# A fused decoder layer on one core: the product with the inverted softmax sums moves from GpSimd to VectorE, and every engine's order is written anew

## The reference, cut to what matters

```
x = layernorm(x + self_attention(x))          # causal; scores from Q, W_cross, shift_weights and gate
x = layernorm(x + cross_attention(x, ctx))    # 112 x 375 scores per head, mask, softmax
x = layernorm(x + ffn(x))                     # ffn: gate, up (256 -> 704), silu(gate)*up, down (704 -> 256)

def fp4_linear(x, w):                         # every linear of the ffn
    return einsum(fp4_quant_dequant(x), fp4_quant_dequant(w))   # blocks of 16: scale = max|x|/6, round to the E2M1 grid
```

## Time and profile before

| what | value |
|---|---|
| median of 3 runs | 675.13 us (674.81 to 675.4) |
| the profiled execution | 676.12 us, of which the span of the core is 674.3 us |
| PE busy | 572.2 us, 85% |
| DVE busy | 537.2 us, 80% |
| ACT busy | 285.4 us, 42% |
| POOL busy | 235.5 us, 35% |
| mean granted TensorE clock | 0.948 of full |
| DMA | 76.95 MB, mean 114 GB/s |

### The profile page before, as it was taken

How to read it: one execution, slowest core, us unless ns; L and a number is a source line. 1 busy time by engine, 2 the same in 40 slices (tenths; PEclk the granted TensorE clock), 3 DMA queues, 4 the chain that set the end, 5 groups by cost and what they waited for, 6 DMA issues and landing times.

```text
span 674.3 us, 15980 instructions
## 1 busy us (share of the span) xinstructions
PE 572.2 (85%) x5410; PEld 360.8 (54%) x5410; DVE 537.2 (80%) x1443; ACT 285.4 (42%) x671; POOL 235.5 (35%) x312
## 2 busy tenths in 40 slices
PE   5876589799989898888989888887989898987875
PEld 3544255355655656565655655564656554544543
DVE  3498688775989979798988979566989887886784
ACT  2442155365345445344444545453444454434312
POOL 5352064352253505243341605242343516133100
PEclk9997699698999999899999989997999999998988
DMA  7566435354453535244452535353453525320000
GB/s 226 143 168 175 128 130 138 95 150 110 105 148 93 153 92 141 72 118 137 120 144 78 149 91 145 111 158 83 115 140 105 142 88 140 83 72 23 29 1 24
DMA packets 75808, 76.95 MB, mean 114 GB/s; under 512 B 13056, under 2 KB 67280, under 8 KB 75728
## 3 DMA queue, kind: packets, MB, share of 16 engines
q1 hardware_dynamic: 73488, 73.58, 40.0%
q10 hardware_dynamic: 2240, 2.35, 1.0%
HBM read 39.72 MB, written 27.00 MB: 99 GB/s over the span
## 4 chain that ended last, share of the span: by engine, by line
PE 40%; DVE 37%; issue 10%; POOL 5%; ACT 3%; DMA 2%; SPq 1%; DVEq 0%; POOLq 0%; ACTq 0%
PE misc L2251 14%; DVE junk L1447 5%; PE misc L2237 4%; PE score L2171 4%; PE prob L2185 4%; PE xpv L2226 3%; DVE qt L1359 3%; DVE qt L1363 3%; PE misc L2337 3%; DVE qt L1353 3%; DVE qt L1361 3%; DVE amax L1439 3%; DVE qt L1356 2%; POOL rstd L752 2%; PE prob L2180 2%
## 5 line engine op out<-in xcount | busy, mean ns | idle before, releaser
L1447 DVE CUSTOM_DVE_ANT_0 junk<-score,maskbias 112x375 bf16<-112x375 f32 x256 | 129.3, 543 | 57.1 <-PE score L2171 56.8
L947 ACT ACTIVATE xP<-prob 128x448 f32<-128x448 f32 (+1 forms) x192 | 95.2, 540 | 90.3 <-PE prob L2185 86.5
L2251 PE MATMUL misc<-wguT,xqT 128*128 128x352 f32 x224 | 81.7, 497 | 1.8 <-ACT xqT L907 1.1
L748 POOL TENSOR_TENSOR aattT<-anum,aden 128x224 f32<-128x224 f32 x16 | 10.6, 665 | 204.9 <-DVE aden L1486 196.1
L728 POOL TENSOR_TENSOR move_a<-mT,negeye 16x448 bf16<-16x448 f32 x64 | 63.5, 1014 | 48.5 <-ACT mT L907 48.5
L728 POOL TENSOR_TENSOR move_x<-mT,negeye 16x448 bf16<-16x448 f32 x64 | 61.2, 971 | 54.7 <-ACT mT L907 54.7
L752 POOL TENSOR_TENSOR rstd<-veps,half 128x1 f32<-128x1 f32 (+1 forms) x44 | 27.1, 621 | 108.1 <-DVE veps L1522 108.1
L2171 PE MATMUL score<-xK,xQ 64*128 64x375 f16 x256 | 45.6, 348 | 17.6 <-DVE xmax L1447 16.6
L2251 PEld LDWEIGHTS misc<-wguT,xqT 128*128 128x128 f32 x224 | 44.7, 206 | 25.0 <-issue 10.0
L2185 PE MATMUL prob<-move_x,shift_x 128*128 128x448 bf16 x192 | 54.8, 365 | 1.2 <-POOL move_x L728 0.9
L2226 PE MATMUL xpv<-xP,xV 128*32 128x112 f32 (+1 forms) x1536 | 54.5, 273 | 1.0 <-ACT xP L947 0.9
(11 more groups left out here) (157 smaller groups left out, 1094.2 us busy)
## 6 DMA issues: line engine op xcount, KB each, us to landing
xk_dram<-xk_parts SPq DMA_DIRECT2D x64, 192.0 KB, 3.2
xK<-xk_dram SPq DMA_DIRECT2D x16, 768.0 KB, 4.5
ctxT_s<-in_ctxT SPq DMA_DIRECT2D x15, 375.0 KB, 3.5
ak_dram<-ak_parts SPq DMA_DIRECT2D x64, 64.0 KB, 2.2
aq_dram<-aq_parts SPq DMA_DIRECT2D x64, 64.0 KB, 2.1
aK<-ak_dram SPq DMA_DIRECT2D x16, 256.0 KB, 3.0
aQ<-aq_dram SPq DMA_DIRECT2D x16, 256.0 KB, 3.7
xq_dram<-xq_parts SPq DMA_DIRECT2D x64, 64.0 KB, 2.1
```

Of the source, the lines that this page charges most:

```text
L947: act.activation(xP[0:KEYS[c], g % 2, c], prob[m][0:KEYS[c], 0:GH * S].rearrange("p (h q) -> p h q", h=GH), ACT.Exp).then_inc(probs.taken[ ...
L1447: dve.tensor_tensor_reduce(junk[:, m], score[m][0:S, 0:SC], maskbias[:], 1.0, -3.0e38, ALU.add, ALU.max, xmax[:, b.par, h:h + 1]).then_inc ...
L2251: mm = pe.matmul(misc[m][0:rows_, 0:cols], actT(c), weightT(c), start=(c == 0), stop=(c == DT - 1))
```

## The change

Two things are changed. First, `attend` becomes a function of the VectorE block. It is the same instruction with the same operands and waits; it follows `invert` of the same batch after some other work, 16 times for self and 16 times for cross attention:

```
-            def attend(b, n):                       # in the gpsimd block
-                ...
-                pool.wait_ge(inverted[n], b.times(1, 1))
-                pool.tensor_tensor(dst, num[n][:], den[n][:], ALU.mult).then_inc(att_ready[n], 1)
+            def attend(b, n):                       # in the vector block
+
+                if n == 0:
+                    if b.c > 0:
+                        miscs.wait_full(dve, Batch(b.c - 2), "A.o")
+                        dve.nop(nofuse=True)
+                    dst = aattT[:]
+                else:
+                ...
+                dve.wait_ge(num_in[n], b.times(32, 32))
+                dve.nop(nofuse=True)
+                dve.wait_ge(inverted[n], b.times(1, 1))
+                dve.tensor_tensor(dst, num[n][:], den[n][:], ALU.mult).then_inc(att_ready[n], 1)
```

Second, the calls in `ramp()`, `slot(i)` and `drain()` of all five engines stand in another order, and the lists of the PSUM rings with them. Of the slot's ring:

```
-MISC_ORDER = ["v", "k", "q", "hT1", "hT0", "A.mT", "down", "X.xT", "gate0", "up0", "gate1", "up1", "K0", "A.o",
-              "V0", "K1", "V2", "V1", "X.o", "A.xT", "X.mT", "A.q"]
+MISC_ORDER = ["v", "q", "k", "hT1", "hT0", "A.mT", "down", "X.xT", "gate0", "up0", "gate1", "up1", "K0", "A.o",
+              "V0", "K1", "V2", "V1", "X.mT", "A.xT", "X.o", "A.q"]
```

More of the change, by code:

```diff
@@ L581, in ramp @@
[L581 to L591 removed]
+                next_x(at[1])
+                put_k(at[2], at[4])
@@ L776, in ramp @@
                 diagonal(at[-1], at[0], 3, False)
-                attend(at[0], 0)
                 residual(at[0])
+                power(0, at[0])
+                shifts(0, at[0])
+                keep_x1(at[0])
                 diagonal(at[0], at[1], 0, False)
@@ L782, in ramp @@
                 diagonal(at[0], at[1], 3, False)
-                power(0, at[0])
-                shifts(0, at[0])
-                keep_x1(at[0])
                 residual(at[1])
-                attend(at[1], 0)
+                residual(at[2])
                 power(0, at[1])
@@ L1235, in slot @@
                 ctxv(i, kv, 1)
+                maxima(i, 1, "X.mT")
                 take(i, "A.xT", x1T[:])
-                maxima(i, 1, "X.mT")
+                if ft:
+                    layernorm(ft, 2, y[:, ft.par])
                 xq_hi_(i, a)
@@ L1797, in slot @@
+                moments(at[3], at[1], 1, "X.o", 2)
             def slot(i):
@@ L1826, in slot @@
                 max_cross(i, c, 1)
+                if ft:
+                    moments(i, ft, 2, "down", 0)
                 max_cross(i, c, 2)
@@ L1829, in slot @@
                     gate_(i, f, 0)
+                if ft:
+                    moments(i, ft, 2, "down", 1)
+                if f:
                     up(i, f, 0)
@@ L1939, in drain @@
+                layernorm(at[11])
+                up(at[14], at[10], 0)
+                quant_x(at[11], 0)
+                quant_h(at[14], at[10], 0, 0)
+                quant_x(at[11], 1)
+                quant_x(at[11], 2)
+                quant_x(at[11], 3)
+                moments(at[14], at[9], 2, "down", 1)
+                quant_x(at[11], 4)
                 gate_(at[14], at[10], 1)
                 up(at[14], at[10], 1)
+                quant_h(at[14], at[10], 1, 0)
+                max_cross(at[15], at[15], 0)
@@ new lines, in drain @@
+                max_cross(at[15], at[15], 1)
+                moments(at[14], at[9], 2, "down", 2)
+                quant_x(at[11], 5)
+                max_cross(at[15], at[15], 2)
+                quant_x(at[11], 6)
+                max_cross(at[15], at[15], 3)
+                quant_h(at[14], at[10], 0, 1)
+                quant_x(at[11], 7)
+                max_cross(at[15], at[15], 4)
+                quant_h(at[14], at[10], 0, 2)
+                quant_h(at[14], at[10], 1, 1)
+                max_cross(at[15], at[15], 5)
@@ L2061, in drain @@
                 quant_h(at[17], at[13], 0, 1)
+                moments(at[16], at[11], 2, "down", 2)
                 quant_h(at[17], at[13], 1, 1)
@@ L2644, in drain @@
+                ctx_v(at[14], at[15], 2)
+                turn_max(at[14], at[14], "X.mT", xmax)
+                turn_hq(at[14], at[9], "hT0", range(4))
+                turn_x1(at[14], at[15])
+                turn_xq(at[14], at[10])
                 project_q(at[14], at[15])
                 project_cross(at[14], at[11])
-                turn_max(at[14], at[14], "X.mT", xmax)
+                gate_up(at[14], at[10], "gate", 0)
+                down(at[14], at[9])
+                turned_cross(at[15], at[14], 0, 0)
```

1097 lines of the change are left out of this document (524 added, 573 removed), and 10 rows, old and new, of tables (MISC_IN, SCORE_IN).

## The result

The changed kernel takes 651.88 us (median of 4 runs, 651.08 to 654.14) against 674.97 us of the kernel before on the same chip: 0.967 of the time, 95% interval 0.964 to 0.971. The forecast was 650.0 us. The number came out; three of its terms did not, and they cancelled each other.

The account below looks back on a forecast made before the run. Bound: a chain that changes engines, with PE pausing for DVE and POOL. Steady slots 19.1, ramp 4 and drain 2 sum to 25 us off 676.1: 651, median 650; range 643 to 659 (52%), two in ten outside 638 to 667.

Parts of the forecast that it names:

- Start of the slot: DVE's rounding ahead of xq: three slowed steps become fast, 1.9 us less 0.4, net 1.5 us from PE's 2.01 us pause.
- Steps 4, 5 and 6: 256-wide rounding steps of quant_x on DVE, slowed under POOL's diagonals; forecast to take 0.3, 0.2 and 0.4 us.
- so the 1.62 us hold later steps: Slot start: the 1.62 us from last maximum to diagonals would hold later rounding steps, step 6 starting at 1.2 us.
- End of the slot and product: Steps around xq_parts give back 0.9 us; two products moved from POOL to DVE cost DVE 0.66 us a slot.
- the three items: End of slot (+0.9), product on DVE (-0.66) and PE's xattT pause, mostly taken by a new wait for turn_x1: booked at zero.
- The clock: PE's granted clock falls to 0.50 behind the 2.01 us pause; four long slots shorten by 1.4 us each, 5.6 us.
- Slot 10 has no `quant_x` and gives nothing: Steady slots: slot 10, without that rounding, was booked at no gain; the nine others gave 19.1 us.
- slower: Rival, slot start: delayed diagonals make PE wait there; 0.9 us a slot lost, about 684 us; chance 7%.
- PE has the down projection to do meanwhile: Slot start: this work covers PE while diagonals start later, by 1 us of work put ahead; only 0.4 us charged.
- Ramp and drain: Time before and after the steady slots: 4 us gained in the ramp (bounds +4 to -12), 2 in the drain.
- More comes: Rival, slots: 2.5 us gained per slot rather than 1.5, and the ramp's clock rises; about 638 us; chance 14%.
- The port takes it back: Rival, slots: each cross product on DVE waits 0.96 us for a diagonal, gain 0.5 a slot; 665 us; chance 23%.

Follow-up runs that it names:

- e3: Changed kernel with the last two self maxima on DVE again ahead of the layernorm's output and rounding steps 0 and 1: 650.56 us, ratio 0.963.
- e11: Kernel before with only the layernorm's output and rounding steps 0 and 1 put ahead of the last two self maxima on DVE: 668.65 us, ratio 0.997.
- e13: Changed kernel with DVE's last two self maxima first again and ACT's copy of the turned maxima early again: 653.73 us, ratio 0.970.
- e14: Changed kernel with the start of the slot as before on DVE, ACT and PE (value products in old order): 659.47 us, ratio 0.977.
- e2: Changed kernel with only the product put back on POOL: 662.89 us, ratio 0.980.
- e5: Kernel before with only the first head of each diagonal written in slots 4 to 13, leaving that computation out: 645.84 us, ratio 0.967.
- e10: Kernel before with only xq_parts moved ahead of three roundings in DVE's slot: 672.96 us, ratio 1.006.
- e1: Kernel before with only the product moved to DVE, right behind the reciprocal of the same batch: 673.62 us, ratio 1.000.
- e4: Changed kernel with the first pair of cross scores on PE behind the transposes of xq again: 652.70 us, ratio 0.965.
- e12: Kernel before with layernorm and steps 0 and 1 ahead of the last self maxima, xq_parts earlier, ACT's copy late: 665.44 us, ratio 0.987.

## Why the prediction was right in its number, and wrong in three terms

*Start of the slot.* Steps 4, 5 and 6 took 0.29, 0.23 and 0.43 us, 7 and 8 took 1.04 and 1.04, near what was said (0.3, 0.2, 0.4, 1.0, 0.8), and the pause at xq went. The step "so the 1.62 us hold later steps" was wrong as a reason. The interval from the last maximum to the diagonals is no constant: 1.5 us after, 2.5 in e3, 0.7 in e11. It is set by what stands ahead of the turn on PE and of the copy on ACT, and the ACT move, which I had listed in the change and priced at nothing, is part of it (e13). The start, with steps 5 and 6 caught again and step 4 still fast, is worth 1.1 us a slot (e14), where the forecast had 1.5.

*End of the slot and product.* The step that failed is the one that books the three items "together at zero". The forecast gave a slot 1.5 us and it gained 3.2: 37.7 to 34.5. The pauses at xq_parts (0.86), at xattT (0.76) and at xmax (0.41, which I did not even name) went, and only 0.61 us at turn_x1 (for xV) came, the new wait that the forecast named. I had set the product's 0.66 us on DVE against them, but DVE's time is no cost where it no longer stands ahead of PE. The product took 0.39 us a piece (0.33 expected); its place on DVE is worth 0.5 us a slot (e2). If the parts add up, that leaves 3.2 - 1.1 - 0.5 = 1.6 us. Of it the 0.86 us at xq_parts are contention, since e5 closes that pause and leaves the ones at xattT and xmax. Which single moves of the end bring the 1.6 us was not separated, and e10 shows that moving xq_parts alone does not.

*The clock.* Four long intervals of seven became short: 4 x 1.4 = 5.6 us, as said; every ordinary window stands at 1.00. The four are this profile's: e1, with the same pause of 2 us, has two such intervals of seven. Over the whole span the clock did not rise (0.948 before, 0.944 after).

*Slots 10 and 11.* "Slot 10 has no `quant_x` and gives nothing" should have been -4.15 us. In slot 11 PE waits at move_a instead of at xq, as in the rival "slower". Against it stood "PE has the down projection to do meanwhile", which slot 11 lacks. The condition was read for the usual slot and not for the one where its cover is gone. But the pauses as such do not make the loss. In the two windows PE's time outside its work is 10.0 us after and 10.7 before; its work is 65.3 us after and 60.4 before, at about as many matmuls (651 against 649), at granted clocks of 0.90 and 0.87 against 1.00 and 0.91. The loss is PE's work at the lower clock, and its size is one profile's: e3 and e4, the changed kernel but for one exchange each, take 73.7 and 73.0 us here and not 75.3.

*Ramp and drain.* 1.85 and 0 us came, of 4 and 2. In the first hundred us PE did 71.8 us of work against 70.4 before, and the clock of 50 to 100 us stayed at 0.76. Slot 4's first maximum came at 185.97 us against 187.17 before: the forecast's 185 for the old ramp was 2 us low. The 1.85 us are less than one and the same ramp varies.

The sum: the forecast's 19.1 was for nine slots, and only seven lie in ordinary intervals (7 x 1.5 + 5.6 = 16.1). Of the other two, slot 11 lies in the windows around slot 10 and the start of slot 4 ahead of the first mark. So 27.6 (forecast 16.1) - 4.15 (forecast +1.5) + 1.85 (forecast 4 + 1.5) + 0 (forecast 2) = 25.3, forecast 25.1. The number is right because +11.5 met -5.65, -3.65 and -2, and that was luck.

*The rivals.* "More comes" was the truth of the ordinary slot (2.5 priced, 3.2 came) and was given 14%. "The port takes it back" did not come: of 32 products two met a diagonal, both in the ramp. One took 1.12 us; DVE, then POOL:

```profile
150.03 1.12 DVE L1470 TENSOR_TENSOR xattT<-xnum,xden 128x224 f32<-128x224 f32 x1
```

```profile
149.69 1.21 POOL L728 TENSOR_TENSOR move_x<-mT,negeye 16x448 bf16<-16x448 f32 x1
```

It ends 0.25 us behind that diagonal. By the rule of the Trainium skill (SBUF — State Buffer, "Who interferes with whom") the instruction that issues first keeps the shared ports for its whole length and the other waits; this row agrees. The other product that met one, a self product, for which the forecast had ruled that out, was not held up, and the diagonals were, two of them 2.58 us against 1.8 to 1.9 elsewhere. DVE, then POOL:

```profile
140.29 0.38 DVE L1470 TENSOR_TENSOR aattT<-anum,aden 128x224 f32<-128x224 f32 x1
```

```profile
138.87 2.58 POOL L728 TENSOR_TENSOR move_x<-mT,negeye 16x448 bf16<-16x448 f32 x2 [11.63 <-ACT mT L873]
```

In all ten slots the cross product meets POOL's x1rows instead, which also reads SBUF. It starts inside it and takes 0.38 us, while x1rows takes 1.84 us in nine of them and 1.65 in the tenth, against 1.21 to 1.57 in the same slots before. POOL before, then after:

```profile
256.32 1.22 POOL L719 TENSOR_SCALAR x1rows<-res,mv,rstd 112x256 f32<-112x256 f32 x1
```

```profile
283.59 1.84 POOL L719 TENSOR_SCALAR x1rows<-res,mv,rstd 112x256 f32<-112x256 f32 x1
```

So the rule's cost is seen, but in these rows the instruction that starts later in the trace is not always the one that waits; what decides it was not measured. What failed in the rival is that in the slots the product meets no diagonal, and that where it meets x1rows it is POOL that pays, and no pause of PE comes of it.

## What to carry to other kernels

Where two engines block each other as here, the gain lies in their relative position, and 0.1 us can decide whether a step is caught (0.08 in e12, against 0.29 to spare after). Follow the chain that starts the blocking instruction (here amax, turn on PE, copy on ACT, diagonal) as closely as the one that starts the blocked one. Price a slot by the sum of the bounding engine's pauses, all of them, and ask for each where it will go when the one ahead is closed: in a tight chain it moves on (e10), and it closes only when what makes the chain late is removed, as in e5. Then read the odd slots separately, where the work that covers a wait is missing.

## What the runs showed of the hardware

In e5 a blocked step was not let in at the first change between short instructions of POOL. There the four diagonals take 1.40 us together, some 0.35 each, and step 4, which lasts 0.29 us alone, took 1.03 us, about three of them; POOL, then DVE:

```profile
263.09 1.40 POOL L728 TENSOR_TENSOR move_a<-mT,negeye 16x112 bf16<-16x112 f32 x4 [3.77 <-ACT mT L907]
```

```profile
263.24 1.03 DVE L1356 TENSOR_SCALAR qt<-qt 128x256 uint16<-128x256 uint16 x1
```

Between the diagonals of 0.96 us each step does get in once. POOL pays too: its x1rows, with DVE's work of the new order beside it, takes 1.66 us on the mean of 16 against 1.38 before. And TensorE's granted clock did not follow the pauses alone. Behind the pause of 2.01 us before it fell to 0.50 in four of seven ordinary intervals. It stayed at 1.00 in all ordinary intervals of e10 and e12, with pauses of up to 1.27 us, but of e11's seven, all with a pause of 1.24 or 1.25 us, one (506.46 to 545.05) fell to 0.50 behind it. The 0.87 window of slot 11 holds pauses of 0.87, 0.93 and 0.71 us that end within 2.4 us, and the clock stands at 1.00 at 438 and at 0.50 at 440 us.
